# Products with v in two groups of 512 columns a pass in place of four of 256, in a fused two-layer block on one core

## What is computed

```
q, k, v = split(xn @ w_qkv.T)          # 32, 4 and 4 heads of 64
q, k = rope(q), rope(k)                # k, v repeated 8 times over the heads
scores = where(causal, q @ k.T / 8, min)
attn = softmax(scores)
out = (attn @ v).reshape(b, 256, 2048) @ w_o.T
x = x + out + ffn(xn)
```

## Time and profile before

| | |
|---|---|
| three runs, us | 386.6, 388.68, 385.39 (median 386.6) |
| the profiled execution, us | 387.23 |
| its span (first to last instruction), us | 385.4 |
| PE busy | 369.0 us (96%) |
| DVE busy | 307.1 us (80%) |
| ACT busy | 250.0 us (65%) |
| POOL busy | 279.4 us (72%) |
| the 384 hi and 192 lo matmuls of `heads_out` (L1287) | 76.4 and 54.1 us busy |

### The profile page before, as it was taken

The page is one execution under the profiler, slowest core; times in us unless marked ns, Lnnn a source line. Parts: engine busy times, 40 slices in busy tenths (PEclk is TensorE's granted clock), DMA queues, the critical chain, the costliest instruction groups (busy, mean ns, idle before and its releaser), DMA issues.

```text
span 385.4 us, 8456 instructions
## 1 busy us (share of the span) xinstructions
PE 369.0 (96%) x2888; PEld 343.6 (89%) x2888; DVE 307.1 (80%) x684; ACT 250.0 (65%) x804; POOL 279.4 (72%) x238
## 2 busy tenths in 40 slices
PE   8998889989999998999999999999999999999995
PEld 3667779979899997999999999999999999998985
DVE  6878999876999885779777888787788879788882
ACT  1368855573987764667667676757666667767671
POOL 3437759789999996977779897667997777776000
PEclk9999999999999999899999999999999999999999
DMA  7996112513444345443345643334565343333300
GB/s 261 414 408 284 27 30 55 138 43 81 110 99 96 79 108 130 112 109 80 87 110 120 157 110 92 93 92 98 131 149 142 93 104 83 84 83 86 79 2 27
DMA packets 34219, 45.15 MB, mean 117 GB/s; under 512 B 5505, under 2 KB 25986, under 8 KB 33794
## 3 DMA queue, kind: packets, MB, share of 16 engines
q1 hardware_dynamic: 34032, 44.62, 43.1%
q10 hardware_dynamic: 146, 0.00, 0.0%
HBM read 13.14 MB, written 1.05 MB: 37 GB/s over the span
## 4 chain that ended last, share of the span: by engine, by line
PE 67%; POOL 15%; DVE 9%; SPq 3%; DMA 2%; ACT 2%; issue 2%; POOLq 0%
PE bank L1287 14%; PE bank L1250 11%; PE bank L1307 10%; PE bank L1004 10%; PE bank L1200 10%; PE bank L1253 3%; POOL woT_lo L606 3%; POOL rope_a L669 2%; POOL split_lo L670 2%; POOL split_hi L668 2%; POOL rope_b L660 2%; PE bank L1013 2%; DMA wq0T<-in_L_attn_w_qkv_dram 2%; PE bank L1159 2%; POOL rope_a L658 2%
## 5 line engine op out<-in xcount | busy, mean ns | idle before, releaser
L515 ACT ACTIVATE bank<-bank,neg_max 128x256 f32<-128x256 f32 (+1 forms) x256 | 101.3, 397 | 10.0 <-DVE neg_max L911 9.9
L524 ACT ACTIVATE probT_hi<-bank 128x512 fp32r<-128x512 f32 x96 | 57.6, 600 | 73.6 <-PE bank L1004 73.4
L911 DVE TENSOR_REDUCE neg_max<-bank 128x2 f32<-128x512 f32 (+1 forms) x96 | 65.9, 687 | 31.2 <-PE bank L1253 30.9
L1287 PE MATMUL bank<-probT_hi,v 128*128 128x256 f32 x384 | 76.4, 295 | 0.6 <-DVE oT_lo L939 0.6
L660 POOL TENSOR_TENSOR rope_b<-turned,cst 128x512 f32<-128x512 f32 x36 | 47.1, 1308 | 40.6 <-DMA turned<-raw 40.6
L1250 PE MATMUL bank<-kT,qT 128*128 128x256 f32 (+1 forms) x512 | 73.4, 276 | 1.7 <-DMA qT<-split_lo 1.7
L927 DVE TENSOR_TENSOR prob<-bank,rsum 128x512 f32<-128x512 f32 x96 | 66.4, 691 | 3.3
L1250 PEld LDWEIGHTS bank<-kT,qT 128*128 128x128 f32 x512 | 66.5, 191 | 1.9 <-DMA qT<-split_lo 1.9
L933 DVE TENSOR_TENSOR probT_lo<-bank,probT_hi 128x512 fp32r<-128x512 f32 x96 | 65.4, 681 | 0.5 <-ACT probT_hi L524 0.4
L1287 PEld LDWEIGHTS bank<-probT_hi,v 128*128 128x128 f32 x384 | 58.6, 189 | 3.5 <-issue 2.2
L1004 PE MATMUL bank<-cst,prob 128*128 128x128 f32 x384 | 58.4, 275 | 2.2 <-DVE prob L927 2.2
(11 more groups left out here) (158 smaller groups left out, 735.2 us busy)
## 6 DMA issues: line engine op xcount, KB each, us to landing
turned<-raw SPq DMA_DIRECT2D x144, 64.0 KB, 2.0
qT<-split_hi SPq DMA_DIRECT2D x64, 128.0 KB, 2.4
qT<-split_lo SPq DMA_DIRECT2D x64, 128.0 KB, 2.4
wq0T<-in_L_attn_w_qkv_dram SPq DMA_DIRECT2D x4, 512.0 KB, 7.9
wout<-in_L_attn_w_out_dram SPq DMA_DIRECT2D x4, 512.0 KB, 12.4
nat_qkv<-in_L_attn_w_qkv_dram SPq DMA_DIRECT2D x2, 1024.0 KB, 20.5
nat_o<-in_L_attn_w_o_dram SPq DMA_DIRECT2D x1, 2048.0 KB, 21.4
kT<-split_hi SPq DMA_DIRECT2D x16, 128.0 KB, 2.4
```

The costliest lines, as they stand in the source:

```text
L515: ins = nc.scalar.activation(own, own, ACT.Exp, bias=neg_max[it % 2][:, first + j:first + j + 1], accum_out=sums[it % 2][:, first + j:firs ...
L524: nc.scalar.activation(probT[0][:, n % 4, :], bank[2 + n % 2][:, :], ACT.Copy).then_inc(t_hi, 1)
L911: dve.tensor_reduce(neg_max[n // UNITS % 2][:, unit_columns(n % UNITS)], score_bank(n)[:, :].rearrange("p (h k) -> p h k", h=heads), AX.X, ...
L1287: ins = pe.matmul(group_bank(), v[b % 2][:, DH * z:DH * z + P], p, start=m == 0, stop=m == last)
```

## The change

`unit_heads` orders the halves of a pass 0, 1, 1, 0, 1, 1. The products with v are two groups: units 0 and 3 (half 0, eight heads), six matmuls of 512 columns, and units 1, 2, 4, 5 (half 1, eight heads), twelve matmuls of 512 columns. Both run in the next pass, on PE in its slots 0 and 2 (`GROUP_AT`), and their results are copied out in its slots 1 and 3 (`TAKEN_AT`); there are two copies on ACT and two on DVE a pass, of 512 columns. In ACT's slot the copy stands right behind `probs_T`, in DVE's right behind `maxima`. Both halves of `project_out` stand in slots 4 and 5 (before: 1 and 5). The q projection of slot 0 moves to slot 1, the k and v projections of slot 4 to slot 5. `probT` holds six units in two buffers, and `oT` is single. In the diff the first `slot` is ACT's, the lines with `maxima` and `heads_lo` are DVE's, those with `project_out` PE's.

```
-            c, h = ((1, 0), (1, 2), (0, 0), (0, 4), (1, 4), (1, 6))[u]
+            c, h = ((0, 0), (1, 0), (1, 2), (0, 4), (1, 4), (1, 6))[u]
...
-        GROUPS = ((0, 1), (2,), (3,), (4, 5))
+        GROUPS = ((0, 3), (1, 2, 4, 5))
...
-        GROUP_AT = {4: (0, 0), 5: (0, 1), 0: (-1, 2), 2: (-1, 3)}
+        GROUP_AT = {0: 0, 2: 1}
+        TAKEN_AT = {1: 0, 3: 1}
...
-            if u == 0 and it + 1 < ITS:
+            if u == 1 and it + 1 < ITS:
                 return [("q", it + 1, 1)]
-            if u == 4 and g == 1 and b + 1 < B:
+            if u == 5 and g == 1 and b + 1 < B:
                 return [("k", b + 1)]
...
             def slot(n):
                 if 2 <= n < N_UNITS + 2:
                     probs_T(n - 2)
+                if group_at(n, TAKEN_AT):
+                    heads_hi(*group_at(n, TAKEN_AT))
                 if n < N_UNITS:
                     probs(n)
-                if group_at(n):
-                    heads_hi(*group_at(n))
...
                 if n < N_UNITS:
                     maxima(n)
+                if group_at(n, TAKEN_AT):
+                    heads_lo(*group_at(n, TAKEN_AT))
                 if 1 <= n < N_UNITS + 1:
                     normalise(n - 1)
                 if 2 <= n < N_UNITS + 2:
                     probs_lo(n - 2)
-                if group_at(n):
-                    heads_lo(*group_at(n))
...
-                pe.wait_ge(o_done, it * 4 + 2 + 2 * half)
+                pe.wait_ge(o_done, it * 2 + 2)
...
-                if it and u in (1, 5):
-                    project_out(it - 1, u // 5)
+                if it and u >= 4:
+                    project_out(it - 1, u - 4)
...
+            project_out(ITS - 1, 0)
             project_out(ITS - 1, 1)
```

More of the change, by code:

```diff
@@ L136, in build @@
         prob = [at(f"prob{i}", 56 * K + 2 * K * i, [P, 512]) for i in range(3)]
-        probT = [at(f"probT_{w}", k * K, [P, 4, 512], F32R) for w, k in (("hi", 104), ("lo", 112))]
+        probT = [[at(f"probT{c}_{w}", k * K, [P, 2 + 2 * c, 512], F32R) for w, k in (("hi", k_hi), ("lo", k_lo))]
+                 for c, k_hi, k_lo in ((0, 64, 68), (1, 104, 112))]
         yT_full = at("yT_full", 156 * K, [P, B, 512])
@@ L274, in unit_columns, with group_at, group_place, turned_place @@
             return slice(8 * c + h, 8 * c + h + heads)
-        GROUPS = ((0, 1), (2,), (3,), (4, 5))
+        GROUPS = ((0, 3), (1, 2, 4, 5))
         GROUP_OF = {u: i for i, us in enumerate(GROUPS) for u in us}
-        GROUP_AT = {4: (0, 0), 5: (0, 1), 0: (-1, 2), 2: (-1, 3)}
+        GROUP_AT = {0: 0, 2: 1}
+        TAKEN_AT = {1: 0, 3: 1}
         def score_bank(n):
             return bank[BANKS_S[n % 3]]
[L286 to L297, removed]
+        def group_at(n, table):
+            it, i = n // UNITS - 1, table.get(n % UNITS)
+            return (it, i) if i is not None and 0 <= it < ITS else None
+        def group_place(i):
+            return [w[:, :, P * i:P * i + P] for w in oT]
         def group_bank():
-            return bank[BANK_O][:, 0:2 * P].rearrange("p (j q) -> p j q", q=P)
+            return bank[BANK_O][:, :].rearrange("p (j q) -> p j q", q=P)
+        def turned_place(n):
+            i = GROUP_OF[n % UNITS]
+            return [w[:, GROUPS[i].index(n % UNITS), :] for w in probT[i]]
         def v_blocks(par):
@@ L521, in probs_T @@
                 act.wait_ge(t_full, n + 1)
-                if n >= 4:
-                    act.wait_ge(pv_done, (n - 4) // UNITS * 4 + GROUP_OF[(n - 4) % UNITS] + 1)
-                nc.scalar.activation(probT[0][:, n % 4, :], bank[2 + n % 2][:, :], ACT.Copy).then_inc(t_hi, 1)
+                if n >= UNITS:
+                    act.wait_ge(pv_done, (n // UNITS - 1) * 2 + GROUP_OF[n % UNITS] + 1)
+                nc.scalar.activation(turned_place(n)[0], bank[2 + n % 2][:, :], ACT.Copy).then_inc(t_hi, 1)
             def heads_hi(it, i):
-                act.wait_ge(pv_done, it * 4 + i + 1)
-                nc.scalar.activation(group_place(it, i)[0], group_bank(), ACT.Copy).then_inc(o_hi, 1)
+                act.wait_ge(pv_done, it * 2 + i + 1)
+                nc.scalar.activation(group_place(i)[0], group_bank(), ACT.Copy).then_inc(o_hi, 1)
             def slot(n):
@@ L570, in _ @@
                     slot(n)
-            for n in range(sum(map(len, SLOTS_AT.values())), N_UNITS + 3):
+            for n in range(sum(map(len, SLOTS_AT.values())), N_UNITS + 4):
                 slot(n)
@@ L1282, in heads_out @@
                             if chunks == 1:
-                                p = probT[s][:, units[0] % 4, :].rearrange("p (h q) -> p h q", q=P)[:, odd:4:2, :]
+                                p = probT[0][s][:, :, :].rearrange("p u (h q) -> p (u h) q", q=P)[:, odd:8:2, :]
                             else:
-                                at_unit = units[0] % 4
-                                p = probT[s][:, at_unit:at_unit + 2, P * (2 * odd + k):P * (2 * odd + k) + P]
+                                p = probT[1][s][:, :, P * (2 * odd + k):P * (2 * odd + k) + P]
                             ins = pe.matmul(group_bank(), v[b % 2][:, DH * z:DH * z + P], p, start=m == 0, stop=m == last)
```

23 lines of the change are left out of this document (11 added, 12 removed).

## The result

The changed kernel takes 420.17 us (median of 4 runs, 417.95 to 421.41). The kernel before, on the same chip, takes 386.00 (4 runs, 385.28 to 388.68). The ratio is 1.087, with a 95% interval of 1.084 to 1.090: slower, by 34 us. The profiled execution is the run of 417.95 us; its span is 416.1, which is 30.7 over the span of before.

What follows compares the result with a forecast made beforehand. TensorE (PE) was taken as the bound; changes at the start, in the passes and in the tail summed to +29.3 us on the 385.4 us span, 414.7, plus 1.8 around it: 416.5, stated as 416, range 408 to 424.

Steps and rivals of the forecast that it cites:

- Only PE's own work counts: Products with v, every pass: half as many, at 0.233 us spacing, save only 0.08 us a pass, 1.2 us over 16 passes.
- The loop: Slots 1-2 and 3-4: transposes to transposes through head copies and `normalise` 3.30 us, PE's own work 2.48, wait 0.82 each.
- The 0.24 of the second group: Slot 2: the group of four units waits for `probs_lo`, starting 0.60 instead of 0.36 us after the transposes.
- Pass 1: Pass 1, 20.04 us before: 20.43 plus 0.5 kept of its earlier excess, a change of +0.9 us.
- Pass 3: Pass 3, 21.02 us before: 19.01 plus 1.5 kept of the 3.6 for the qT wait and slow clock, -0.5 us.
- Pass 15: Pass 15, 15.72 us before: likewise 19.01, a change of +3.3 us.
- the rival with the falling clock: Every pass: the clock falls, about 1.9 us each, 30 over sixteen passes, 446 us in all; chance 0.06.
- Tail: Behind pass 15: both groups and both halves of the last projection follow, +5.1 us, with 0.9 for the clock +6.0.
- The 0.9 for the clock: Tail: 0.9 us added for a slower clock behind 2.7 us of PE idle time.
- the loop closes in time: Rival, slots 2 and 4: loop under 2.48 us, passes 17.13 and 18.55, 386 to 388 us in all; chance 0.04.
- in only one of two slots: Rival, slots 2 and 4: only one of the two waits per pass is real, 403 us in all; chance 0.05.
- a wide product costs hardly more than a narrow one: Rival, products with v: at 0.119 us each a pass loses 2.05 us, 383 us in all; chance 0.02.

Runs made afterwards that it cites:

- e4: The changed kernel with each 512-column product with v issued as two of 256, 36 matmuls a pass instead of 18: 422.61 us, ratio 1.094.
- e8: e7 with the last transposes ahead of the first tail group and the last group in its own bank, not waiting for copies: 388.26 us, ratio 1.007.
- e1: The changed kernel with `heads_lo` moved behind `normalise` and `probs_lo` on DVE, `heads_hi` still early on ACT: 396.82 us, ratio 1.026.
- e3: The kernel before with only the head copies moved early, `heads_hi` behind `probs_T` and `heads_lo` behind the maxima: 419.67 us, ratio 1.086.
- e2: e1 with `heads_hi` also moved behind the exponentials on ACT, so both head copies stand last: 417.84 us, ratio 1.082.
- e7: e5 with the q projection of pass 0 alone back in slot 0, as in the kernel before: 390.88 us, ratio 1.012.
- e5: e1 with `heads_lo` on DVE behind `probs_lo` in slot 1 only, and between `normalise` and `probs_lo` in slot 3: 394.07 us, ratio 1.020.

## Why the prediction was right

The sign and the size came out: 416 predicted, 420.17 measured, inside the range, and the cause is the one that was named. Step by step:

- **Only PE's own work counts.** Right. The wide products start 0.23 us apart: in the last section's rows of the tail, three of them take 406.66 - 405.97 = 0.69. The gain of width was small, as said, but mis-sized: 0.08 a pass and 1.2 in all were said, e4 puts it at 0.2 and 2.7, and the spacing of 0.229 at 0.16 a pass. The 131 ns of the Trainium skill (TensorE: Matmul & The Clock Gate, Back-to-back issue gap) is not seen in any run here; by it PE would have about 18 x 0.10 = 1.8 us less to do in e8's ordinary pass of 17.28, which is an estimate from the page's figure.
- **The loop.** Right to 0.01 us: 3.31 where 3.30 was summed. The rows show 0.68 and 0.66 us of idle time where 0.82 was said. The difference is only in how PE's own work is counted: 0.82 is 3.30 less the 2.48 of spacings, while the row's idle time begins at the modelled end of the mask product, at 249.63, 2.63 behind the first transposes. The distance from transposes to transposes is what the sum gave. The pass, 19.00 to 19.04, is the 19.01 of the sum, and 20.47 the 20.43. That the place is the cause was only argued then. e1 shows it by taking `heads_lo` out of the loop (19.00 to 17.39) and e3 by adding early copies to the kernel before. The 0.24 of the second group is not the loop's: in e8, without the loop, the group stands 0.58 behind its transposes too. The loop itself costs 19.00 - 17.28 = 1.7 us a pass. What the prediction did not see is that the old places cost as much with the wide groups (e2).
- **Pass 1 was mis-sized.** Said 20.43 + 0.5 = 20.93, measured 22.51. The wait of 1.58 us for qT lies ahead of this stretch, in that of pass 0; I had let the delay of the q projection in there (-0.8, measured 103.21 to 102.52 = -0.7). What I had left out is the slow clock behind the wait. Slots 0 and 1 of pass 1, of the changed kernel and of e1, whose wait was 1.25:

```profile
102.52:109.55 7.03, 7.03 (x41) 6.29 (x42) 5.24 (x9) 4.41 (x15) 6.95 (x7) 0.76 0.44 103
102.14:107.60 5.46, 5.46 (x41) 5.08 (x41) 5.22 (x12) 4.58 (x16) 5.38 (x5) 1.00 0.21 51
```

The same 41 matmuls take 7.03 us at a granted clock of 0.76 and 5.46 at 1.00: 1.57, all of the 1.58 that was missing.
- **Pass 3 was mis-sized the other way.** Said 20.5, of which 1.5 was a rest of the wait for qT; measured 19.04, no wait at all. PE asked for this q at 155.74; in e1 it came at 155.34. So the loop, which delays PE, hid the wait, and e1 shows how long it is without that: 3.11 us. The two errors cancel, by luck.
- **Pass 15 was mis-sized.** Said 19.01, measured 20.63. Without a projection to do there, PE idles 2.11 us ahead of the transposes at 386.51, and the clock falls. I counted the idle time and not what the clock does behind it; the rival with the falling clock had this mechanism, but for each pass, where the granted clock stays at 1.00.
- **Tail.** Said 10.64 + 6.0 = 16.6, measured 15.76. The length without the clock was right (15.7, loop of the end 3.10 where 3.09 was summed, half 0 of the projection 9.49 behind the transposes of unit 94 where 9.39 was said). The 0.9 for the clock did not come in this execution; in e7, whose tail has the same groups, copies and projections, it did (17.04 at 0.87). One step of the sum had a piece without a term: 1.85 + 3.09 + 12 x 0.233 is 7.74 and not 7.99. The rows have the last product's end at 8.08 (409.83 - 1.41 - 400.34), so it did no harm.
- **Rivals.** That the loop closes in time, or in only one of two slots, is excluded by the 30 waits of passes 1 to 15. That a wide product costs hardly more than a narrow one is excluded by its spacing.
- **Span against median.** The sum was made against one execution and gave a span of 414.7, measured 416.1. So 1.4 of the 4 us by which 416 is short are errors of the terms. The rest is mostly that the profiled run is the lowest of the four, 2.2 under their median. Its mean granted clock is 0.992, that of the other three 0.984 to 0.988, so the slow stretches that the sum left out weigh more in them.

What stays open: how the end of e3 became 7.7 us longer, and why the clock falls in some places (below).

## What to carry to other kernels

An engine's own queue is part of the dependence chain. Before moving an instruction forward on a queue, write down who waits for it and who waits for those that it now stands ahead of, and sum the way round from the bounding engine back to itself; share of busy time (here 73% and 59%) says nothing about it. Here `heads_lo` stood ahead of `normalise`, which PE asks for first, and that alone was 26 us. Moving everything back to the end is no cure: with `heads_hi` last as well, the copies came too late and it cost as much (e2). And a slow loop hides other late work: once it is gone, look again for what it covered (here a DMA chain, 3 us), and count what a coarser grouping pushes into the tail, since that is paid in full.

## What the runs showed of the hardware that was not expected

Idle time alone doesn't tell when TensorE's clock falls. Behind 1.58 us (102.52) and 2.11 us (386.51) in the changed kernel and 3.11 us in e1 it fell to the lower level. Behind 2.10 us in pass 14 and 2.50 us in the tail of the changed kernel it did not, as the timeline of PE and the spacing behind them show:

```profile
375.30 0.66 PE L1006 MATMUL bank<-cst,prob 128*128 128x128 f32 x4 [2.10 <-DVE prob L929]
376.04 0.40 PE L1308 MATMUL bank<-woT_hi,oT_lo 128*128 128x256 f32 x2
376.28 0.40 PE L1308 MATMUL bank<-woT_lo,oT_hi 128*128 128x256 f32 x2
...
405.40 0.73 PE L1288 MATMUL bank<-probT_hi,v 128*128 128x512 f32 x2 [2.50 <-DVE probT_lo L935]
405.97 0.40 PE L1288 MATMUL bank<-probT_lo,v 128*128 128x512 f32 x1
406.20 0.62 PE L1288 MATMUL bank<-probT_hi,v 128*128 128x512 f32 x2
406.66 0.39 PE L1288 MATMUL bank<-probT_lo,v 128*128 128x512 f32 x1
```

Nor does the length of a wait at one and the same place tell. Ahead of the first scores of pass 1, 1.46 us in e4 and 1.58 in the changed kernel were followed by a lower clock (granted 0.63 from 102.67 to 107.30, 0.76 in the rows above), and 1.56 us in e2 was not (1.00 from 102.65 to 108.10). Ahead of the last group PE waits 2.10 us in e1, e2, e5 and e7; behind it the granted clock was 1.00 in e1 and e5 and 0.65 in e2 and e7. Two waits of 0.66 and 0.68 us in each of the passes 1 to 13 of the changed kernel never brought it down. In pass 15 the fall cost 20.63 - 19.01 = 1.6 us. No run here separates what decides it.
